# Third pass of a two-layer graph kernel: the message one-hots of every even slot written by one VectorE comparison instead of eight ScalarE squares and a relu

## What is computed

```python
feat_src = (feat @ W2s + b2s).reshape(n, H, F)
feat_dst = (feat @ W2d + b2d).reshape(n, H, F)
en = feat_src[src]
ev = feat_dst[dst]
e = leaky_relu(en + ev, 0.2)
e = sum(e * attn, axis=-1)
m = segment_max(e, dst)
ee = exp(e - m[dst])
alpha = ee / max(segment_sum(ee, dst)[dst], 1e-9)
msg = softmax(en * r_feat * alpha, axis=-1)        # r_feat: 200000 x 2 x 32
g_sum = sum(segment_sum(msg, dst), axis=1)
rst = (feat + g_sum) @ W1 + b1
```

## Time and profile before

| | us |
|---|---|
| median of 3 runs | 5373.82 |
| lowest, highest | 5369.94, 5382.69 |
| profiled execution, its span | 5453.1 |

### The profile page before, as it was taken

One profiled execution on the slowest core, in us unless ns is written; L12 is line 12 of the kernel. 1 busy time (PEld: TensorE's weight loads), 2 busy tenths in 40 slices (PEclk: granted clock), 3 DMA queues, 4 the chain that ended last, 5 costly groups with the idle time before them and its releaser, 6 DMA issues. The chain is left out here.

```text
span 5453.1 us, 78876 instructions
## 1 busy us (share of the span) xinstructions
PE 3477.0 (64%) x26045; PEld 2492.3 (46%) x26045; DVE 2315.1 (42%) x6794; ACT 2934.3 (54%) x7797; POOL 2940.4 (54%) x2955
## 2 busy tenths in 40 slices
PE   5777887777667777767644456555554555655655
PEld 3444444444344444445544344444444544544544
DVE  8655444334311111111522444645445446446467
ACT  5665655555533333334200176677666677776775
POOL 4654554455344444444466655565555665665646
PEclk9898888888877777777755566666666676666668
DMA  3443443334355555555333344344433443443432
GB/s 96 155 154 153 154 154 132 150 129 154 149 190 181 167 176 173 171 168 186 106 76 77 80 103 108 101 114 105 104 98 101 108 119 104 115 105 98 122 106 82
DMA packets 347736, 698.55 MB, mean 128 GB/s; under 512 B 125562, under 2 KB 207540, under 8 KB 339417
## 3 DMA queue, kind: packets, MB, share of 16 engines
q1 hardware_dynamic: 257168, 620.81, 33.2%
q0 software_dynamic: 88192, 72.56, 8.4%
q10 hardware_dynamic: 1969, 0.10, 0.0%
HBM read 437.19 MB, written 255.99 MB: 127 GB/s over the span
## 5 line engine op out<-in xcount | busy, mean ns | idle before, releaser
L1943 POOL DMA_INDIRECT gath<-fs_scratch,src_idx x1564 | 1542.2, 986 | 996.9 <-issue 464.4
L896 ACT ACTIVATE scratch<-sum_x_ps_c 128x600 bf16<-128x600 f32 (+7 forms) x1003 | 775.4, 826 | 537.0 <-PE sum_x_ps_c L933 362.6
L833 POOL DMA_INDIRECT gath<-in_x,src_idx x620 | 665.6, 1074 | 652.2 <-PE sum_x_ps_s L986 457.6
L2068 ACT ACTIVATE scratch<-scratch,bias,weight 128x32 f32<-128x32 f32 x2608 | 943.9, 400 | 131.8 <-issue 130.9
L2005 PE MATMUL ps_m<-scratch 128*64 128x128 f32 x2880 | 596.0, 368 | 480.7 <-issue 379.5
L833 POOL DMA_INDIRECT gath<-y_scratch,src_idx x540 | 522.4, 967 | 599.8 <-PE sum_y_ps_s L986 424.1
L2005 PEld LDWEIGHTS ps_m<-scratch 128*64 128x64 f32 x2880 | 487.2, 192 | 549.1 <-issue 506.3
L2149 DVE SCALAR_TENSOR_TENSOR scratch<-ps_e,attn_sb 128x128 f32<-128x128 f32 x784 | 188.7, 284 | 1178.7 <-remote 1013.8
L1985 PE MATMUL ps_e<-fdw,scratch 128*128 128x66 f32 x3136 | 527.8, 333 | 237.5 <-issue 159.6
L933 PE MATMUL sum_x_ps_c<-e_tab,scratch 128*128 128x300 bf16 (+7 forms) x2006 | 526.7, 351 | 221.4 <-ACT scratch L896 123.7
L1985 PEld LDWEIGHTS ps_e<-fdw,scratch 128*128 128x128 f32 x3136 | 528.2, 252 | 289.4 <-issue 176.4
(11 more groups left out here) (306 smaller groups left out, 4826.7 us busy)
## 6 DMA issues: line engine op xcount, KB each, us to landing
count_scratch<-scratch SPq DMA_DIRECT2D x58, 3200.0 KB
scratch<-count_scratch SPq DMA_DIRECT2D x232, 800.0 KB
en_scratch<-gath SPq DMA_DIRECT2D x196, 264.0 KB
onehot<-rel_scratch SPq DMA_DIRECT2D x196, 256.0 KB
scratch<-in_edge_attr_2x SPq DMA_DIRECT2D x390, 128.0 KB, 2.7
scratch<-en_scratch SPq DMA_DIRECT2D x180, 264.0 KB
gath<-fs_scratch,src_idx POOLq DMA_INDIRECT x1564
fdw<-fd_scratch SPq DMA_DIRECT2D x392, 33.0 KB
```

The lines of the kernel that those rows point to most:

```text
L833: pool.indirect_dma_start(out=gath[:, s, t, 0:F], out_offset=None, in_=table_dram, in_offset=bass.IndirectOffsetOnAxis(ap=src_idx[:, g, k: ...
L896: act.activation(to, ps_c[u % pairs][:, :, 0:q].rearrange("p h (d a) -> p h a d", d=d), ACT.Copy).then_inc(kept, 1)
L1943: pool.indirect_dma_start(out=gath[:, s, t, :], out_offset=None, in_=fs_dram, in_offset=bass.IndirectOffsetOnAxis(ap=src_idx[:, g, k:k + 1 ...
L2068: e = act.activation(rows, rows, ACT.Exp, bias=bias[:, q, i:i + 1], scale=weight[:, q, i:i + 1], accum_out=total[:, q, i:i + 1] if i < K * ...
```

## The change

The rule which slots have their message one-hot made by DVE gets a second part: besides every third of the last slots, all even slots from 2 to 162. For them ACT's eight squares and relu fall away, and DVE does the one comparison that it does for the last slots. The counts on which PE and ACT wait follow the rule, in two functions instead of one. The comparison's wait for an earlier sum is left out in the first steps, where there is none yet.

```diff
-            def by_vector(n, turn):
-
-                return sum(on_vector(i, turn) for i in range(n + 1)) if isinstance(n, int) else 0
-
             def onehot_on_vector(n):
-                return on_vector(n, 0)
+
+                return on_vector(n, 0) or (0 < n <= TAIL and n % 2 == 0)
+
+            def onehots_by_vector(n):
+
+                return sum(onehot_on_vector(i) for i in range(n + 1))
+
+            def scaled_by_vector(n):
+
+                return sum(scaled_on_vector(i) for i in range(n + 1))
...
                         if scaled_on_vector(n - 2):
-                            pe.wait_ge(msg_vector, by_vector(n - 2, 1))
+                            pe.wait_ge(msg_vector, scaled_by_vector(n - 2))
                         else:
-                            pe.wait_ge(msg_ready, n - 1 - by_vector(n - 2, 1))
+                            pe.wait_ge(msg_ready, n - 1 - scaled_by_vector(n - 2))
                         if onehot_on_vector(n - 2):
-                            pe.wait_ge(oh_msg_vector, by_vector(n - 2, 0))
+                            pe.wait_ge(oh_msg_vector, onehots_by_vector(n - 2))
                         else:
-                            pe.wait_ge(oh_msg_ready, n - 1 - by_vector(n - 2, 0))
+                            pe.wait_ge(oh_msg_ready, n - 1 - onehots_by_vector(n - 2))
...
                     far.then_inc(distant, 1)
-                    act.wait_ge(distant, n + 1 - by_vector(n, 0))
+                    act.wait_ge(distant, n + 1 - onehots_by_vector(n))
...
                     if exists(n, 1) and onehot_on_vector(n - 1):
-                        dve.wait_ge(summed, n - 2)
+                        if after(n, 3):
+                            dve.wait_ge(summed, n - 2)
                         dve.tensor_tensor(
                             oh_msg[:, q1 % 2, :, :], wide(iota[:, :], 1, [P, ST, WINDOW]),
```

## The result

| | before | after |
|---|---|---|
| median on one chip, 4 runs each, us | 5371.88 | 5296.56 |
| lowest, highest, us | 5319.96, 5382.69 | 5283.39, 5314.27 |
| profiled execution, its span, us | 5453.1 | 5295.4 |
| start of the third pass's first gather, us | 2684.3 | 2627.4 |

What follows compares the result with a forecast made beforehand. The third pass was taken as bound by waits around POOL's bursts. 9 more long cycles (40 us) plus 13 us in softmaxes, 53 us, gave 5506 against the profiled span, 5427 us after carrying over the median's difference; range 5315 to 5500.

Steps and rivals of the forecast that it cites:

- part (3): DVE's comparison between L2158 and L2172 starts the even sum 1.15 us later, turning short cycles long at 4.4 us each.
- from 4.8 us on always long: Third pass: an even sum starting 4.8 us or more into POOL's burst is always followed by a long pause.
- the creep of the earlier trace: Third pass, profile before: even sum's start drifted from 2.9 to 4.9 us into the burst in three cycles, then 8.09 us pause.
- The comparison blocks gathers: Rival: each of the 81 comparisons lengthens a burst by its own 1.15 us; 106 us slower, 5480 us, chance 0.05.
- ACT was the pace: Rival: without ACT's even squares the creep may stop and long cycles turn short; 5334 us (5277 to 5361), chance 0.33.
- Part (1): ACT loses eight squares and a relu per even slot, 290 us in all, mostly beside other work; worth at most 26 us.
- Part (4): In long cycles DVE's 2 to 6 us of slack covers the comparison; without that cover, 1.15 us per cycle.
- Part (5): In softmax stretches DVE is the bound and nothing covers the comparison: 11 x 1.15 = 13 us.
- Part (6): DVE's added wait on summed, from the third step on, costs nothing; uncovered, up to the odd sum's delay in a burst.
- Part (7): PE's changed wait counts cost nothing; ACT's exponentials may start up to 3.6 us earlier, given nothing, 26 us at most.
- starts at 3.6 us stay stable: Sign of being wrong: even sums hold that start because the creep came from ACT alone; long pauses fewer than 20.
- gathers beside L2164 over 1.3 us: Sign of being wrong the other way: POOL's gathers beside DVE's new comparison take longer than 1.3 us.

Runs made afterwards that it cites:

- e6_before_again: The kernel before, unaltered, profiled a second time beside other runs; the kernel before took 5370 us on that chip.
- e5: The changed kernel, unaltered, run again on another chip against the kernel before: 0.977.
- e2: The kernel before with only DVE's comparison added for even slots 2 to 162, result unread, ACT's work kept: 0.979 of before.
- e1: The changed kernel without its 81 new comparisons, those even one-hots not made at all, so only ACT's relief: 0.992 of before.
- e7: The kernel before with a one-input DVE reduction, result unread, added in the comparison's place for even slots: 1.002 of before.
- e14: The changed kernel with the 81 comparisons reading iota from a copy in PSUM instead of SBUF: 0.996 of before.
- e3: The changed kernel with ACT's even-slot squares and relu done again into a buffer nobody reads: 0.981 of before.

## Why the prediction was wrong

**The rhythm and the time scale were right.** Bursts of 20.2 us, two kinds of pause, and the store behind SP's wait as what makes a pause long: what the two profiles differ by is mainly 16 long pauses fewer (10 fewer against `e6_before_again`). 89 us by 16 pauses is 5.6 us each, more than the 4.4 I took, since the short pauses fell too (3.4 us now against 3.6).

**The step that failed** is part (3) of the change, in the sentence before it already: "So what decides a cycle is when the even sum starts", with limits of 3.7 and 4.8 us. The starts moved as forecast, to 3.6 and 4.0, the ends to 7.3 and 7.7. But the limit is not a fixed time in the burst. Of the bursts of 16 gathers that began with an even slot and whose sum started 3.5 to 4.2 us in, none of 126 ended in a long pause in the three kernels with the comparison (after, e5, e2), and 30 of 52 did in the three that hold up no gather at that place (e1, e7, e14). In 11 of these 52 the third gather came more than 0.2 us late all the same, and none of the 11 ended in a long pause. The same start thus goes with either pause, and what decides is whether one of the first gathers comes late. My forecast of 9 long pauses more (40 us) became 16 fewer. The limit itself, "from 4.8 us on always long", did not hold even in the trace of before: of 15 such bursts with a start after 4.8 us, 4 ended in a pause of 3.3 to 4.9 us. One is the burst that follows the creep of the earlier trace rows, from 3761.27. Its sum starts 5.0 us in, but POOL's second gather comes 2.8 us after the first, and the pause is short:

```profile
3764.07 0.94 POOL L1943 DMA_INDIRECT gath<-fs_scratch,src_idx  x1 [1.86 <-issue]
...
3766.26 3.67 PE L2005 MATMUL ps_m<-scratch 128*64 128x128 f32 x16
...
3769.00 0.69 DVE L2190 TENSOR_TENSOR scratch<-scratch,total 128x512 f32<-128x512 f32 x1
3769.07 1.44 POOL L1943 DMA_INDIRECT gath<-fs_scratch,src_idx  x1 [0.31 <-issue]
...
3786.38 0.95 POOL L1943 DMA_INDIRECT gath<-fs_scratch,src_idx  x1 [3.29 <-remote]
...
4759.48 0.69 DVE L2124 TENSOR_TENSOR scratch<-scratch 128x512 f32<-128x512 f32 x1
```

Of all 42 bursts of 16 gathers that began with an even slot there, 14 had the third gather more than 0.2 us late, and 1 of them ended in a long pause; of the other 28, 12 did. I had seen a correlation within one kernel and used it as a law, without asking what else differed between the cycles. e7 is the case where it would have held: a delay and no hold-up of its own, 38 long pauses in its slowest execution. Yet even there the median was only 0.2% higher, not told from zero.

**The rule and the row.** I let one row, L2190, which held up no gather, speak for the comparison, and I read it wrongly. The gather at 4758.40 had begun 0.47 us before L2190 (4758.87), so it came first. The one that took 1.33 us began at 4759.65, while L2124 ran (4759.48 to 4760.17, last line above), and ended 0.81 us after it; L2092, to which I put it, began only at 4760.08. L2190 holds up gathers like the others: the one at 3769.07 began 0.07 us after L2190 had begun (3769.00) and ended at 3770.51, 0.82 us after the end of L2190. In the trace of before, between 3100 and 5050 us, all 39 gathers that began while L2190 ran (by the measure used for the comparison) ended 0.82 us after it, and so did 21 of 21 with L2124 and 11 of 11 with L2092; of the 290 that had begun up to 0.9 us before one of the three, none did. The Trainium skill, page "SBUF — State Buffer", section "Who interferes with whom", says that a DVE instruction with two inputs in SBUF contends with GpSimd's reads, that one with a single SBUF input, outside certain modes, does not, and that whoever comes second fully blocks. The trace agrees: L2190, L2124 and the comparison from SBUF block the gather that comes second, the reduction of e7 and the comparison with iota in PSUM block none. Whether L2092, with one input, ran in one of those modes no run shows. The same section also says that a tensor_tensor did not stall DMAs in a probe; the gathers here, DMAs that POOL issues, were stalled, and the measurement decides.

**The rival that came nearest in its mechanism was priced with the wrong sign.** "The comparison blocks gathers" had 5480 us, since I let each of 81 gathers lengthen the pass by 1.15 us. The hold-up was 0.55 us in the mean, the gathers of slots 34 to 162 grew by 7 us in all, as fewer gathers now begin while L2190, L2124 or L2092 runs (12, from 71), and the side effect was worth over ten times that. **"ACT was the pace"** gave 5277 to 5361, which holds the measured time, but e2 and e3 show that it is not the reason. Part (1) with "at most 26 us" (0.5%) was of the right size: nothing that shows where the gathers are held up, 0.4 to 1.2% where they aren't (e1).

**The smaller steps.** The comparison takes 1215 ns in the loop, not 1150, and 98 us in all for the 81. Part (4), its cover in long cycles, can't be told apart any more, since few are left. Part (5), 2 to 3 us longer softmax stretches: four slots took 64.5 us before (from 3786.4) and 65.6 after (from 3701.7), the four slots of the next softmax 66.5 and 64.7, so it cost nothing that shows. Part (6), the added wait: L2170 sat idle 0.4 us in all, as forecast. Part (7): ACT's relus of the odd slots ran ahead, but as the relief is worth nothing, so is this. The 13 us for the softmaxes in the sum thus had no counterpart. Of the signs I named, "starts at 3.6 us stay stable" came true, but the cause behind it, a creep from ACT alone, did not; and "gathers beside L2164 over 1.3 us", meant as the sign of a loss, came true too, as the sign of the gain.

## What to carry to other kernels

A limit read from one trace ("a sum that starts after 4.8 us is late") needs a look at the cycles that break it, and at what else the change does inside the burst, before a forecast rests on it. When two engines block each other, one row without a delay proves nothing until it is clear which of the two began first. When one engine issues transfers back to back and the others crawl under it, a gap of half a microsecond early in the burst can be worth more than it costs, and costs one instruction to try. And test the cost side of a change alone: here it gave as much as the whole change (0.979 against 0.977 to 0.981).

## What the runs showed of the hardware

- A gather that began while a DVE comparison of 128x1024 with both inputs in SBUF ran ended 0.82 us after it (53 of 53 in the kernel after). The same holds for a tensor_tensor of 128x512 from SBUF (60 of 60 before, L2190 and L2124) and for L2092's tensor_scalar (11 of 11). A gather that had begun first ran through (none of 325 held up). With one input in PSUM (e14) or as a reduction (e7) the DVE instruction held up none of 30 and none of 21.
- In the kernel before, once POOL had issued its first gathers back to back at 1.25 us, the end of a sum could reach SP 15 us late (burst from 3732.80: 8.3 us into it, SP going on at 22.9), and PE issued one matmul in 2.1 us. With the second gather held up by 0.3 to 0.8 us, signals of sums that ended by 8.0 us still came at once in most bursts (54 of 59). What is shared there, and why the gap moves it, no run shows; that stays open.
- The same kernel took 5370 to 5527 us on different chips, and the gain was 1.2% on the chip of the result, 2.3 and 2.0% on two others.
